# A two-layer decoder on one core: scores for the row maxima on 32x32 tiles of the TensorE array

## The chip, the cores and the metric

The kernel runs on one core of one Trainium2 chip. The metric is the device time of that core in microseconds (us); lower is better. Everything is one program, launched once. TensorE (PE in the profile) multiplies matrices, VectorE (DVE), ScalarE (ACT) and GpSimd (POOL) do the elementwise work, and SyncE (SP) issues DMAs.

## The reference

The input x is 8 sequences of 256 tokens with 512 features. It passes six sublayers, each followed by a layer norm of the sum with its input. Three of them hold causal softmax attention with small heads, and these are the ones that matter here:

```
# layer 0, differential attention: 32 heads of 16 features, keys shared in groups
scores = einsum('bhqd,bhkd->bhqk', q, k) * 16 ** -0.5
scores = where(causal, scores, min);  probs = softmax(scores)
# layer 1, attention: 16 heads of 32 features
scores = einsum('bhqd,bhkd->bhqk', q, k) * 32 ** -0.5      # causal, softmax
# layer 1, last sublayer: 16 query heads of 32 features against one shared key per token
att = einsum('bhqd,bkd->bhqk', q, k_shared) / sqrt(32)     # causal, softmax
```

The other three are a long convolution, a mixture of 8 experts (top 2), and cross attention with 512 features.

## The kernel before

The program has a front stage (layer 0's attention, up to about 460 us), a convolution stage, a middle stage and an experts stage (to about 1199 us), and a tail stage (all of layer 1).

In the front and the tail a softmax is computed in two rounds. First the scores are computed with queries as rows, masked, and VectorE takes the maximum of every row. These maxima are then split into bfloat16 parts, turned, and subtracted by a matmul inside a second computation of the scores, with keys as rows (`scoreT`), whose result ScalarE exponentiates. The first computation serves the maxima alone. It is done by `score(b, n)` in the front, six units for each of the 8 sequences, and by `score(kind, b, c)` in the tail, four units for each sequence in each of two attentions ("P" and "A"), 64 units in all.

A unit fills a PSUM tile `scores` of four banks, `[128, 4, 512]`. Each bank g belongs to one row strip of the array: 32 partitions of q and k, which hold one head (or two of 16 features). Four such strips, each with an operand of 32 partitions, can be in the array side by side, and each writes its own bank. A unit has two steps:

1. `add_masks` (L115 to L123) writes the causal mask with 16 bfloat16 matmuls, for column strip j and row strip g: 32 partitions in, 32 rows out, 256 columns (512 in the front's units n of 4 and 5). This is a tiling of the array in 32x32.
2. The scores are added by fp32 matmuls of 32 partitions in and 128 rows (queries) out, one for each row strip g, a tiling in 32x128. In the front, units n below 4 have four of 512 columns (L335), and units 4 and 5 have two times four of 256 columns (L341). In the tail each unit has four of 256 columns (L1883) and four of 128 (L1886).

The trace has two weight loads and two matmul records for every fp32 matmul of the program, the two passes; a bfloat16 matmul has one of each. Below, a pair is one weight load with its matmul record.

The order of TensorE's work is written out by hand. Between two units stands other work, projections above all (`cols`, `rows`, `query`, `key`; helpers at L191 and L198). The one `scores` tile is claimed through `quads`: a unit waits until VectorE's maxima of the unit before are done (L770 and L774 in the front, L2603 and L2604 in the tail).

Of the kernel before, what the change touches and what calls it, by code (L numbers as in the profile page):

```python
# [13 lines left out]
P = 128  # L14
B = 8
S = 256
# [98 lines left out]
def add_masks(pe, consts, out, copies):  # L115


    for j in range(4):
        for g in range(4):
            rows = slice(32 * g, 32 * g + 32)  # L120
            at = WEDGE + 32 * (g - j)
            part = consts["wedge"][rows, at:at + P].unsqueeze(1).to_broadcast([32, copies, P])
            pe.matmul(out(g, slice(32 * j, 32 * j + 32)), consts["ident_bf"][rows, rows], part, start=True, stop=False,  # L123
                      skip_group_check=True)
# [81 lines left out]
def front_stage(nc, consts, x_in, ctx_in, base_out, vT, cT, w, norm_w, skip, spare, filters, pad_stored, first_traffic, expand, next_traffic,  # L206
# [11 lines left out]
    with ExitStack() as ctx:  # L218
# [62 lines left out]
        def strip(g):  # L281
            return slice(32 * g, 32 * g + 32)
# [13 lines left out]
        with nc.Block() as block:  # L296
            @block.tensor
            def _(pe):
                def drained(key):
                    pe.wait_ge(ring.drained_sem(key), ring.count(key))  # L300
# [24 lines left out]
                def score(b, n):  # L325
                    if n == 0:
                        for j in range(4):
                            drained(("q", b, j))
                        drained(("k", b))
                    bank = quads.claim(pe, ("S", b, n))  # L330
                    q, k = qT[b % 2], kT[b % 2]
                    if n < 4:
                        add_masks(pe, consts, lambda g, rows: bank[rows, g, :].rearrange("p (a k) -> p a k", a=2)[:, :, P:S], 2)
                        for g in range(4):
                            ins = pe.matmul(bank[:, g, :], q[strip(g), n, P:S], k[strip(g)].rearrange("p a k -> p (a k)"),  # L335
                                            start=False, stop=True, skip_group_check=True)
                    else:
                        add_masks(pe, consts, lambda g, rows: bank[rows, g, :].rearrange("p (a k) -> p a k", a=4), 4)
                        for h in range(2):
                            for g in range(4):  # L340
                                ins = pe.matmul(bank[:, g, h * S:(h + 1) * S].rearrange("p (a k) -> p a k", a=2),  # L341
                                                q[strip(g), 2 * (n - 4) + h, 0:P], k[strip(g), :, 0:P], start=False, stop=True,
                                                skip_group_check=True)
                    ins.then_inc(quads.filled_sem(("S", b, n)), 1)

                def shift(b):
# [1373 lines left out]
def tail_stage(nc, consts, region, y_stored, x_in, x_out, y_slots, slot, share, ctx_q, ctx_o, wa, wvo, w, early, early_loaded, cT, ctx_wq, ctx_wo):  # L1720
# [5 lines left out]
    with ExitStack() as ctx:  # L1726
# [87 lines left out]
        def query_of(kind, b):  # L1814
            return q_of.get(b, qT["P"]) if kind == "P" else qT["A"]

        def key_of(kind, b):
            return k_of.get(b, kT["P"]) if kind == "P" else kT["A"]
# [16 lines left out]
        with nc.Block() as block:  # L1835
            @block.tensor
            def _(pe):
                def drained(key):
                    pe.wait_ge(ring.drained_sem(key), ring.count(key))
# [26 lines left out]
                def score(kind, b, c):  # L1866
                    if kind == "P":
                        if c % 2 == 0:
                            drained(("P", "q", b, c // 2))
                            drained(("P", "k", b, c // 2))  # L1870
                        kc = c
                    else:
                        if c == 0:
                            drained(("H", "k4", b))
                        if c % 2 == 0:
                            drained(("H", "q", b, c // 2))
                        kc = 0
                    bank = quads.claim(pe, (kind, "S", b, c))
                    q, k = query_of(kind, b)[:, c], key_of(kind, b)[:, kc]
                    add_masks(pe, consts, lambda g, rows: bank[rows, g, P:3 * P].rearrange("p (a k) -> p a k", a=2), 2)  # L1880
                    for g in range(4):
                        s = slice(32 * g, 32 * g + 32)
                        pe.matmul(bank[:, g, 0:S], q[s, P:S], k[s, 0:S], start=False, stop=False, skip_group_check=True)  # L1883
                    for g in range(4):
                        s = slice(32 * g, 32 * g + 32)
                        ins = pe.matmul(bank[:, g, S:S + P], q[s, 0:P], k[s, 0:P], start=False, stop=True, skip_group_check=True)  # L1886
                    ins.then_inc(quads.filled_sem((kind, "S", b, c)), 1)

                def shift(kind, b):
# [208 lines left out]
                for r in range(2, B):  # L2098
                    p, c, h, a = (r - n if 0 <= r - n < B else None for n in range(4))
# [61 lines left out]
                c, h, a = B - 1, B - 2, B - 3  # L2161
# [74 lines left out]
                for k in range(NC):  # L2236
                    if k < NC - 1:
                        drained(("A", "W", c, k))
                    for t in range(NT):
                        if k == NC - 1:  # L2240
                            pe.wait_ge(half_mixed, t + 1)
                        ins = pe.transpose(banks[t][:, k * P:(k + 1) * P], mixedT[:, k, t * P:(t + 1) * P], consts["ident"][:])
# [746 lines left out]
```

## Time and profile before

| | |
|---|---|
| median of 3 runs | 2129.62 us (2128.32 to 2130.3) |
| span of the profiled execution | 2127.3 us |
| TensorE busy with matmuls | 2057.7 us, 97% of the span |
| TensorE's weight loads | 1194.6 us, 56%, mostly beside the matmuls |
| VectorE | 1128.4 us, 53% |
| ScalarE, GpSimd | 518.8 us, 580.5 us |

The profile is of one execution. A record of a matmul begins when it is let into its part of the array and ends with a modelled end, so records overlap, and the distance from one start to the next start says more than a duration. Tiling and shape stand in a row as `32*128 32x256`: 32 partitions in, 128 rows out, and an operand of 32 partitions by 256 columns that is streamed.

### The profile page before, as it was taken

The numbers are of one execution on the slowest core, as the hardware profiler recorded it, in microseconds if no ns is written. First come the engines' busy times: TensorE is split into PE (matmuls) and PEld (weight loads), VectorE is DVE, ScalarE is ACT, GpSimd is POOL, SyncE is SP. The second block draws the span as 40 slices with busy tenths as digits, with TensorE's granted clock in tenths as the row PEclk, the third lists the DMA queues.
The fourth block names the chain that finished last, engine by engine and source line by source line (L and its number), as shares of the span: only waits on it lengthen the run. The fifth ranks groups of instructions, "written<-read, shape, count | busy, mean of one in ns | idle before, by whom it ended". The sixth has DMA issues, their size and how long they took to land. (4 is left out here: it accounts for less than half of the span.)

```text
span 2127.3 us, 32323 instructions
## 1 busy us (share of the span) xinstructions
PE 2057.7 (97%) x13439; PEld 1194.6 (56%) x13439; DVE 1128.4 (53%) x1731; ACT 518.8 (24%) x791; POOL 580.5 (27%) x548
## 2 busy tenths in 40 slices
PE   7899999999999999999999999999999999999996
PEld 5444444334444557556566655766666666666664
DVE  2567777567777744122222334364646464736567
ACT  2445555440000121101011122122222222222211
POOL 2222222128999600111110312022222222121122
PEclk9999999999999999999999999999999999999998
DMA  5101111205111147321211602100010101000000
GB/s 161 48 1 55 55 56 45 87 38 210 40 43 44 35 156 277 126 65 65 65 65 55 222 3 99 50 31 21 17 44 1 60 1 41 1 31 12 1 11 21
DMA packets 66237, 130.81 MB, mean 61 GB/s; under 512 B 6480, under 2 KB 19920, under 8 KB 66096
## 3 DMA queue, kind: packets, MB, share of 16 engines
q1 hardware_dynamic: 45968, 77.49, 11.1%
q10 hardware_dynamic: 14448, 32.64, 4.3%
q0 software_dynamic: 5680, 18.62, 3.0%
q8 instruction: 111, 1.82, 0.4%
q14 instruction: 30, 0.25, 0.0%
HBM read 97.40 MB, written 41.81 MB: 65 GB/s over the span
## 5 line engine op out<-in xcount | busy, mean ns | idle before, releaser
L1033 PE MATMUL conv_conv<-kv,toep 128*128 128x512 f32 x576 | 247.6, 592 | 0.3 <-POOL kv L1067 0.3
L2615 DVE RECIPROCAL tail_inv<-tail_ring 128x256 f32<-128x256 f32 x63 | 110.7, 1757 | 188.8 <-PE tail_ring L1935 188.3
L1623 PE MATMUL moe_gu_ps<-gu,xT_tile 128*128 x608 | 192.4, 459 | 0.0
L1033 PEld LDWEIGHTS conv_conv<-kv,toep 128*128 128x128 f32 x576 | 109.4, 190 | 139.0 <-issue 129.6
L1067 POOL TENSOR_TENSOR kv<-vT,cT 128x512 f32<-128x512 f32 x128 | 147.0, 1172 | 15.8 <-PE conv_conv L1033 12.0
L2302 POOL TENSOR_TENSOR tail_rstd_x<-tail_rstd_x,const_minus_half 128x2 f32<-128x2 f32 x31 | 21.8, 702 | 469.6 <-DVE tail_rstd_x L2577 469.6
L1623 PEld LDWEIGHTS moe_gu_ps<-gu,xT_tile 128*128 128x128 f32 x608 | 112.3, 190 | 66.5 <-issue 17.8
L2310 POOL TENSOR_SCALAR_AFFINE_SELECT tail_expT<-tail_expT 128x1024 f32<-128x1024 f32 x64 | 71.5, 1119 | 242.1 <-ACT tail_expT L2394 242.0
L2603 DVE TENSOR_REDUCE tail_negtop<-tail_scores 128x4 f32<-128x1024 f32 x64 | 78.2, 1221 | 95.6 <-PE tail_scores L1886 95.4
L594 POOL TENSOR_SCALAR_AFFINE_SELECT front_expT<-front_expT 128x2048 f32<-128x2048 f32 x32 | 64.3, 2008 | 199.1 <-ACT front_expT L649 199.1
L1604 POOL DMA_INDIRECT xg<-x_after,tokens x37 | 35.0, 947 | 282.3 <-PE moe_xT_ps L1618 255.2
L1705 DVE TENSOR_TENSOR moe_hid<-moe_gu_ps,moe_silu 128x352 f32<-128x352 f32 x39 | 20.5, 525 | 170.7 <-PE moe_gu_ps L1623 170.7
L649 ACT ACTIVATE front_expT<-front_scores 128x2048 f32<-128x2048 f32 x48 | 90.1, 1878 | 78.3 <-PE front_scores L367 78.3
L1651 PE MATMUL moe_y_ps<-down,moe_hT 128*128 (+1 forms) x234 | 107.1, 593 | 0.7 <-ACT moe_hT L1691 0.7
L2394 ACT ACTIVATE tail_expT<-tail_scores 128x1536 f32<-128x1536 f32 x63 | 91.4, 1451 | 64.8 <-PE tail_scores L1912 64.8
L1674 ACT ACTIVATE moe_silu<-moe_gu_ps 128x352 f32<-128x352 f32 x39 | 18.1, 464 | 270.2 <-PE moe_gu_ps L1623 270.2
L770 DVE TENSOR_REDUCE front_negtop<-front_scores 128x8 f32<-128x2048 f32 x32 | 73.2, 2288 | 18.6 <-PE front_scores L335 18.4
L2315 POOL TENSOR_TENSOR tail_expT<-tail_expT 128x512 f32<-128x512 f32 x60 | 76.7, 1279 | 5.0
L1089 ACT COPY both<-conv_conv 128x512 f32<-128x512 f32 x32 | 18.7, 586 | 229.9 <-PE conv_conv L1033 211.0
L1717 DVE COPY moe_y<-moe_y_ps 128x512 f32<-128x512 f32 x39 | 27.0, 692 | 72.7 <-PE moe_y_ps L1651 72.7
L198 PE MATMUL tail_ring<-tail_gk,tail_xT 128*128 128x416 f32 (+1 forms) x256 | 63.4, 399 | 1.5 <-ACT tail_xT L2376 1.5
L1651 PEld LDWEIGHTS moe_y_ps<-down,moe_hT 128*128 128x128 f32 (+1 forms) x234 | 41.6, 191 | 38.5 <-issue 38.3
(394 smaller groups left out, 3912.2 us busy)
## 6 DMA issues: line engine op xcount, KB each, us to landing
toep<-toeplitz SPq DMA_DIRECT2D x32, 320.0 KB, 2.9
y_slots<-moe_y ACTq DMA_DIRECT2D x39, 256.0 KB, 2.0
gu<-in_L_ffn_gate_up_proj SPq DMA_DIRECT2D x5, 1408.0 KB, 12.5
toeplitz<-filt_rows SPq DMA_DIRECT2D x8, 768.0 KB
front_e<-in_ctx SPq DMA_DIRECT2D x8, 512.0 KB, 4.7
toeplitz<-filt_rows SPq DMA_DIRECT2D x16, 256.0 KB
x_after<-x SPq DMA_DIRECT2D x8, 512.0 KB, 5.0
tail_x<-x_after SPq DMA_DIRECT2D x8, 512.0 KB, 3.7
```

Source lines behind the costliest of these rows:

```text
L594: pool.affine_select(out=tile, in_=tile, compare_op=ALU.is_ge, fill=0.0, base=0, pattern=[[0, 16], [1, P]], channel_multiplier=-1).then_in ...
L649: act.activation(exp_buf(b, n)[:].rearrange("p g j q -> p g (j q)"), scores[:], ACT.Exp).then_inc(quads.drained_sem(key), 1)
L770: ins = dve.tensor_reduce(negtop[:, 1, n].rearrange("p (g a) -> p g a", a=2), scores[:].rearrange("p g (a k) -> p g a k", a=2), AX_X, ALU. ...
L1033: ins = pe.matmul(bank, toep[p][:, mat * P:(mat + 1) * P], kv[p][:, c].rearrange("p b j i -> p (b j i)"), start=n == 0, stop=n == len(PART ...
L1067: pool.tensor_tensor(kv[p][:, c], tokens_of(c, h), context_of(c, h, 3), ALU.mult).then_inc(kv_ready, 1)
L1623: ins = pe.matmul(gu_ps[:, s % 2, h, 0:HID], (xT if s else mid.xT_first)[:, c, :], wgu[c][:, e, h * HID:(h + 1) * HID], start=c == 0, stop ...
L1651: ins = pe.matmul(y_ps[:, s % 2, :], hT[0:w, n, :], wd[n][0:w, e, :], start=n == 0, stop=n == 2)
L2310: pool.affine_select(out=diagonal, in_=diagonal, compare_op=ALU.is_ge, fill=0.0, base=0, pattern=[[0, 8], [1, P]], channel_multiplier=-1). ...
L2315: pool.tensor_tensor(e[:, 3], e[:, 0], e[:, 2], ALU.add).then_inc(masked[kind], 1)
L2394: act.activation(exp_buf(kind, b, c)[:, 0:3].rearrange("p n g q -> p g n q"), quads.tile(key)[:, :, 0:3 * P].rearrange("p g (n q) -> p g n ...
L2603: dve.tensor_reduce(negtop[:, 1, heads_of(c)], scores[:, :, 0:S], AX_X, ALU.max, negate=True)
L2615: link.after(dve.reciprocal(inv[c % 2][:], bank[:, S:2 * S]))
```

## The change

The scores of step 2 are computed on 32x32 tiles. Each fp32 matmul of 128 queries becomes four of 32 queries each, for column strips j of 0 to 3, with the same streamed operand (the keys) and a quarter of the weights. The order is j outside and g inside, as in `add_masks`. A front unit has 16 matmuls in place of 4 (n below 4) or 32 in place of 8; a tail unit has 32 in place of 8. Masks, `scoreT`, all waits and the work of the other engines are as before.

```diff
                         add_masks(pe, consts, lambda g, rows: ..., 2)
-                        for g in range(4):
-                            ins = pe.matmul(bank[:, g, :], q[strip(g), n, P:S], k[strip(g)].rearrange("p a k -> p (a k)"),
-                                            start=False, stop=True, skip_group_check=True)
+                        for j in range(4):
+                            for g in range(4):
+                                ins = pe.matmul(bank[strip(j), g, :], q[strip(g), n, P + 32 * j:P + 32 * j + 32],
+                                                k[strip(g)].rearrange("p a k -> p (a k)"), start=False, stop=True,
+                                                skip_group_check=True)
...
                         for h in range(2):
-                            for g in range(4):
-                                ins = pe.matmul(bank[:, g, h * S:(h + 1) * S].rearrange("p (a k) -> p a k", a=2),
-                                                q[strip(g), 2 * (n - 4) + h, 0:P], k[strip(g), :, 0:P], start=False, stop=True,
-                                                skip_group_check=True)
+                            for j in range(4):
+                                for g in range(4):
+                                    ins = pe.matmul(bank[strip(j), g, h * S:(h + 1) * S].rearrange("p (a k) -> p a k", a=2),
+                                                    q[strip(g), 2 * (n - 4) + h, strip(j)], k[strip(g), :, 0:P], start=False,
+                                                    stop=True, skip_group_check=True)
...
-                    for g in range(4):
-                        s = slice(32 * g, 32 * g + 32)
-                        pe.matmul(bank[:, g, 0:S], q[s, P:S], k[s, 0:S], start=False, stop=False, skip_group_check=True)
-                    for g in range(4):
-                        s = slice(32 * g, 32 * g + 32)
-                        ins = pe.matmul(bank[:, g, S:S + P], q[s, 0:P], k[s, 0:P], start=False, stop=True, skip_group_check=True)
+                    for j in range(4):
+                        rows = slice(32 * j, 32 * j + 32)
+                        for g in range(4):
+                            s = slice(32 * g, 32 * g + 32)
+                            pe.matmul(bank[rows, g, 0:S], q[s, P + 32 * j:P + 32 * j + 32], k[s, 0:S], start=False, stop=False,
+                                      skip_group_check=True)
+                    for j in range(4):
+                        rows = slice(32 * j, 32 * j + 32)
+                        for g in range(4):
+                            s = slice(32 * g, 32 * g + 32)
+                            ins = pe.matmul(bank[rows, g, S:S + P], q[s, rows], k[s, 0:P], start=False, stop=True, skip_group_check=True)
```

## Rows read from the trace of the kernel before

**Rows 1.** The page: span, and the busy time and instructions of each engine.
```profile
span 2127.3 us, 32323 instructions
PE 2057.7 (97%) x13439; PEld 1194.6 (56%) x13439; DVE 1128.4 (53%) x1731; ACT 518.8 (24%) x791; POOL 580.5 (27%) x548
```
**Rows 2.** Busy time by stretch: PE, PEld, DVE, ACT, POOL, granted clock, DMA share, GB/s.
```profile
0.00:460.00 460.00, 430.43 (x3524) 206.57 (x3525) 286.01 (x361) 213.65 (x274) 99.08 (x91) 0.99 0.20 61
1199.00:2050.00 851.00, 844.25 (x6717) 544.97 (x6715) 440.02 (x714) 193.59 (x275) 177.56 (x165) 1.00 0.10 33
```
**Rows 3.** Timeline of PE, tail unit at 1426 us: start us, length us, line, xcount.
```profile
1426.08 0.33 PE L123 MATMUL tail_scores<-const_wedge,const_ident_bf 32*32 32x256 bf16 x16
1426.34 0.50 PE L1883 MATMUL tail_scores<-tail_kT_a,tail_qT_a 32*128 32x256 f32 x4
1426.66 0.39 PE L1883 MATMUL tail_scores<-tail_kT_a,tail_qT_a 32*128 32x256 f32 x4
1426.87 0.40 PE L1886 MATMUL tail_scores<-tail_kT_a,tail_qT_a 32*128 32x128 f32 x8
1426.98 0.29 PE L1886 MATMUL tail_scores<-tail_kT_a,tail_qT_a 32*128 32x128 f32 x4
1427.20 0.48 PE L191 MATMUL tail_ring<-tail_xT,early_wq 128*128 128x256 f32 x1
```
**Rows 4.** Durations (ns min/median/max) of the masks' and L1883's records, by source line.
```profile
L123 PE MATMUL tail_scores<-const_wedge,const_ident_bf x1024: 264/278/278, 1212.0 to 2097.7; 32*32 32x256 bf16 x171
L1883 PE MATMUL tail_scores<-tail_kT_a,tail_qT_a x256: 374/426/478, 1426.3 to 2098.3; 32*128 32x256 f32 x128
```
**Rows 5.** Timeline of PE, two front units, n of 1 and n of 4.
```profile
237.19 0.33 PE L123 MATMUL front_scores<-const_wedge,const_ident_bf 32*32 32x256 bf16 x16
237.45 1.14 PE L335 MATMUL front_scores<-front_kT,front_qT 32*128 32x512 f32 x8
238.52 1.92 PE L386 MATMUL front_ring<-front_expT,front_v 128*32 128x512 f32 x16
...
249.27 0.43 PE L123 MATMUL front_scores<-const_wedge,const_ident_bf 32*32 32x512 bf16 x16
249.64 1.15 PE L341 MATMUL front_scores<-front_kT,front_qT 32*128 32x256 f32 x16
250.71 0.48 PE L191 MATMUL front_ring<-front_xT,front_wk 128*128 128x256 f32 x1
```
**Rows 6.** Timeline of PE: fp32 on four column tiles, first and second passes.
```profile
2112.06 0.42 PE L1932 MATMUL tail_ring<-tail_expT,tail_v_a 128*32 128x256 f32 x4
2112.30 0.40 PE L1932 MATMUL tail_ring<-tail_expT,tail_v_a 128*32 128x256 f32 x4
```
**Rows 7.** Timeline of PE: a unit after an idle time, with what ended that.
```profile
2056.62 0.33 PE L123 MATMUL tail_scores<-const_wedge,const_ident_bf 32*32 32x256 bf16 x16 [1.01 <-DVE tail_negtop L2604]
2057.41 0.40 PE L1886 MATMUL tail_scores<-tail_kT_a,tail_qT_a 32*128 32x128 f32 x8
```
**Rows 8.** Timeline of PE: first and last of the 12 lines of its densest stretch.
```profile
2108.39 0.86 PE L1932 MATMUL tail_ring<-tail_expT,tail_v_a 128*32 128x256 f32 x16 [0.83 <-POOL tail_expT L2310]
...
2113.16 0.40 PE L1939 MATMUL tail_ring<-tail_expT,tail_ones 128*32 128x128 f32 x8
```
**Rows 9.** Timeline of DVE, then of PE, in the front.
```profile
233.54 0.42 DVE L794 TENSOR_TENSOR front_cross<-front_ring,front_sums 128x256 f32<-128x256 f32 x1 [1.45 <-ACT front_sums L657]
...
234.21 2.29 DVE L770 TENSOR_REDUCE front_negtop<-front_scores 128x8 f32<-128x2048 f32 x1
...
238.92 2.29 DVE L770 TENSOR_REDUCE front_negtop<-front_scores 128x8 f32<-128x2048 f32 x1
...
241.27 0.33 PE L123 MATMUL front_scores<-const_wedge,const_ident_bf 32*32 32x256 bf16 x16 [0.24 <-DVE front_negtop L770]
```
**Rows 10.** Timeline of DVE in the tail, the maxima of one unit.
```profile
1436.96 1.23 DVE L2603 TENSOR_REDUCE tail_negtop<-tail_scores 128x4 f32<-128x1024 f32 x1 [3.02 <-PE tail_scores L1886]
1438.10 0.68 DVE L2604 TENSOR_REDUCE tail_negtop<-tail_scores 128x4 f32<-128x512 f32 x1
```
**Rows 11.** The page: the queue that brings instructions: packets, MB, share.
```profile
q8 instruction: 111, 1.82, 0.4%
```

## The prediction

> **What bounds the kernel now.** I read the page first: TensorE is busy for 97% of the span [rows 1]. Then the windows by stage: in the tail from 1199 to 2050 us it is busy for 844 of 851 us, with VectorE at 440; in the front for 430 of 460 us, with VectorE at 286 [rows 2]. The granted clock is 0.99 to 1.00 in both stretches, the 2.4 GHz level, after unbroken work, and the change takes no work away that could let it fall. So a time that a unit gains on TensorE is a gain of the whole, unless TensorE then stands before a wait. The change touches 48 units in the front and 64 in the tail and nothing else, so the whole question is the length of a unit, and I read one of each kind by the starts of its records.
>
> **A tail unit now** [rows 3]. From the masks' start (1426.08) to the start of the next block (1427.20) it takes 1.12 us:
> - The 16 mask records take 0.33 together and one of them takes 0.28 [rows 3, 4], so their starts lie within 0.05. All 16 tiles run side by side.
> - From the last mask start (1426.13) to the first score record (1426.34): 0.21. This is one pass of the masks, and the emptying of the array before the tiling changes.
> - First passes of L1883 start at 1426.34, second ones at 1426.66: 0.32. Second passes to L1886: 0.21, and this is a pass of 256 columns. So 0.11 of the first interval is weights of 128 columns that nothing covers.
> - L1886's first to its second passes (1426.87 to 1426.98): 0.11, a pass of 128 columns.
> - From there to the next block: 0.22, of which the four starts spread over 0.02, a pass is 0.11, and 0.09 is the array emptying for the next tiling. A masks' pass then also takes 0.21 - 0.09, about 0.11.
>
> **The change part by part.** Removed is the tiling change between masks and scores: 0.09 a unit. Its weights of 128 columns become weights of 32. On four column tiles first passes start 0.24 before second ones [rows 6], so that uncovered weights of 32 columns cost 0.24 - 0.21 = 0.03 and not 0.11; here they can load while the masks stream, so I put them at 0, and 0.03 is the other bound. The columns that are streamed stay the same if all 16 tiles run together: each tile streams what its strip streamed. What is added is pairs. A tail unit has 16 mask pairs and 16 score pairs now; it will have 16 and 64. A front unit with n below 4 goes from 16 and 8 to 16 and 32, one with n of 4 or 5 from 16 and 16 to 16 and 64. In all that is 32 x 24 + 16 x 48 + 64 x 48 = 4608 more pairs to the 13439 that the page shows.
>
> Does the order of the program let 16 tiles run together? For every tile the program gives the first pass, then the second, then goes to the next tile. In the trace the four first passes of L1883 start within 0.50 - 0.48 = 0.02, and the four second ones 0.32 later [rows 3, 4], so a waiting second pass does not hold up the next row strip. The same holds across four column tiles [rows 6]: four starts within 0.02 though each is followed by a waiting second pass. No row has 16 tiles with two passes. I take it that they pass each other there too. Three steps in 0.02 is 0.007 for a tile with two pairs, so 16 tiles start over 0.10, against 0.05 for masks [rows 3]; I take 0.10, as these are fp32, and keep 0.05 as the good end.
>
> The new unit, followed at its last tile:
> - tail: 0.10 spread + 0.11 masks + 0.21 + 0.21 + 0.11 (L1883 twice, L1886's first pass) + 0.20 to the next block = 0.94. Gain 1.12 - 0.94 = 0.18; with a spread of 0.05 it is 0.23.
> - front, n below 4, now 238.52 - 237.19 = 1.33 [rows 5]: 0.10 + 0.11 + 0.43 for 512 columns + 0.52 (0.43 + 0.09) = 1.16, gain 0.17 (0.22).
> - front, n of 4 and 5, now 250.71 - 249.27 = 1.44 [rows 5]: 0.10 + 0.21 + 3 x 0.21 + 0.30 = 1.24, gain 0.20 (0.25).
>
> So 0.18 a unit, and 0.23 at the good end.
>
> **What of it reaches the end.** In the tail VectorE stands idle for 3.02 us before a unit's maxima and waits for TensorE [rows 10], and the maxima themselves take 1.23 + 0.68 us, so they are done long before the next unit claims the tile. Around 2056 TensorE does wait for the maxima [rows 7], but these wait for the scores, so the gain counts there too. All 64 units count: 64 x 0.18 = 11.5 us.
>
> In the front VectorE is nearer. Its cross product starts at 233.54 when ScalarE's sums are there, and the first maxima follow at 234.21, the second at 238.92; TensorE's third unit then waits 0.24 for them [rows 9]. That chain does not move when units 0 and 1 become shorter, so their gain turns into a longer wait at unit 2. From there the maxima wait for the scores or nearly do. I count 3.6 of 6 units in each of six steady sequences, and 11 of the 12 in the first and the last sequence: 33 units, x 0.18 = 5.9 us. The bounds are 24 and 48 units, 4.3 and 8.6 us.
>
> Sum: 11.5 + 5.9 = 17.4 us, from a span of 2127.3 to 2109.9. The median of the runs lies 2.3 above the span, so 2112 us. The good end is 64 x 0.23 + 48 x 0.23 = 25.8 us, 2104. On the other side the gain of this case could be half, 2121.
>
> **Rivals.**
> 1. *Too few pairs a microsecond* (slower). A tail unit now starts 32 pairs in about 0.9 us, also after an idle time, 29 ns a pair [rows 7]; the masks alone start 16 in 0.05, 3 ns a pair. The new unit wants 80 in 0.94, 12 ns a pair, and the turning point is 1.12 / 80 = 14 ns. The densest long stretch has 116 pairs (12 lines) from 2108.39 to 2113.29, 42 ns a pair [rows 8], but there the streams set the pace, so the rows only bound the rate from one side. At 29 ns a tail unit takes 2.3 us, +1.2 x 64 = 77, the front units of 80 pairs +0.9 x 16 = 14, those of 48 pairs stay: 2220. At 20 ns, 1.6 us: +0.48 x 64 + 0.16 x 16, less 0.17 x 22 for the others: +30, 2160. The instructions come by a queue that moved 1.82 MB [rows 11]; a third more pairs make it 2.4 MB, which at 0.4% of the engines is nothing unless a burst outruns it. For the rival: nobody has tried more than 32 such pairs in a row. Against: the 3 ns, also straight after an idle microsecond. Chance 0.15, a third of it below 2150. The Trainium skill (TensorE: Matmul & The Clock Gate, section "Wait — 56ns, not 53.3ns?") says that from one matmul's start to the next there are never less than about 25 ns. By that a tail unit would take 80 x 25 = 2.0 us and the kernel some 2190. The masks' starts in this trace do not agree with it, at 3 ns [rows 3, 4].
> 2. *Order within a row strip* (slower). If a waiting second pass holds up the next column tile of the same row strip, the strip runs first of j=0; second of j=0 with first of j=1; and so on: five intervals where two stood. For L1883 and L1886 together that is 4 x 0.21 + 5 x 0.11 = 1.4 in place of 0.64, so a tail unit is 0.05 + 0.11 + 1.39 + 0.09 = 1.64, +0.5 x 64 = 33. Front: 5 x 0.43 + 0.25 = 2.4, +1.05 x 32 = 34, and 9 x 0.21 + 0.35 = 2.3, +0.8 x 16 = 13. Together +80: 2209. It speaks for it that every row with two passes has four tiles alone; against it that neither four row strips nor four column tiles behave so. Chance 0.12. The same page of the Trainium skill (section "Part 3: Packing small matmuls — row/col tiling") says that matmuls keep their program order in start and end; by that rows 3 could not have four first passes before any second one, so the trace disagrees.
> 3. *Weights no longer covered* (about even). Four weight loads of 0.03 for the column tiles of one strip, one after another and beside no pass, are 0.12, at four passes 0.48, and a unit is 0.94 + 0.48 = 1.4 at worst; a half of that gives 1.18, +0.06 x 64 + 0 in the front, 2133. Places between the forecast and 2145 belong here. Chance 0.13. Rows 6 speak against it, where 0.03 is all that shows.
>
> **How the numbers follow.** Forecast 0.60, at 2112; rivals 0.15, 0.12, 0.13. The range of 2104 to 2150 holds the forecast's 0.60, all of the third rival and a third of the first, 0.78; it reaches no further up, since the next case is at 2160 to 2220. A measurement of this kernel can tell some 0.2% (4 us) from no change. Faster by more: 0.60 and a little of the third, 0.62. Within: 0.08. Slower: 0.30.
>
> **What would show it.** Right: masks and scores of a tail unit start within 0.75 of each other with no gap of 0.2 between L123 and the scores, and the next block starts 0.94 after the masks (0.89 to 0.98). Records of first passes lie on 16 tiles within 0.10. First rival: starts of pairs in even steps of more than 12 ns, and the unit's length proportional to its pairs, so that front units of 48 pairs gain and those of 80 lose. Second: second passes interleave with first passes of the next j at steps of 0.21. In the front the wait at the third unit for the maxima grows from 0.24 to about 0.6. The prediction is wrong if units come out longer than 1.12 in the tail, whatever the reason.

## The result and the profile after

The changed kernel takes 2149.27 us (median of 4 runs, 2144.56 to 2151.27) where the kernel before took 2129.96 in the same session (4 runs). The ratio is 1.0095, with a 95% interval of 1.0082 to 1.0108: it is slower by 19.3 us. The forecast was 2112, a gain of 17.4. The time lies just inside the range of 2104 to 2150, but the sign is wrong.

The page of the changed kernel, the lines that answer to [rows 1, 11]: span, busy time and count of each engine, and the queue that brings instructions.

```profile
span 2146.5 us, 41539 instructions
PE 2078.1 (97%) x18047; PEld 1212.3 (56%) x18047; DVE 1127.5 (53%) x1731; ACT 518.6 (24%) x791; POOL 579.7 (27%) x548
...
q8 instruction: 147, 2.41, 0.5%
```

The pairs grew by 18047 - 13439 = 4608, the number that was counted. The span grew by 19.2 us and TensorE's busy time by 20.4. Its idle time up to its last matmul, all gaps added up, went from 61.6 to 60.3 us. So no new wait for another engine took the gain: units became longer inside. The two stretches say the same as [rows 2], at the same granted clock (columns as there; the stretches are shifted by the later start of the tail, and the first is 10 us longer):

```profile
0.00:470.00 470.00, 440.24 (x5068) 214.34 (x5068) 289.81 (x363) 215.99 (x277) 100.01 (x92) 0.99 0.19 60
1202.00:2069.00 867.00, 860.09 (x9486) 556.17 (x9484) 441.46 (x715) 193.56 (x274) 177.13 (x165) 1.00 0.10 33
```

A tail unit, a front unit with n below 4 and one with n of 4 or 5, in the timeline of PE (start us, length us, line, xcount), to be set beside [rows 3, 5]. L1888 is the old L1883, L1894 the old L1886, L336 and L344 the old L335 and L341:

```profile
1442.20 0.33 PE L123 MATMUL tail_scores<-const_wedge,const_ident_bf 32*32 32x256 bf16 x16
1442.32 0.77 PE L1888 MATMUL tail_scores<-tail_kT_a,tail_qT_a 32*32 32x256 f32 x25
1442.75 0.27 PE L1894 MATMUL tail_scores<-tail_kT_a,tail_qT_a 32*32 32x128 f32 x1
1442.76 0.47 PE L1888 MATMUL tail_scores<-tail_kT_a,tail_qT_a 32*32 32x256 f32 x7
1442.94 0.72 PE L1894 MATMUL tail_scores<-tail_kT_a,tail_qT_a 32*32 32x128 f32 x31
1443.58 0.48 PE L191 MATMUL tail_ring<-tail_xT,early_wq 128*128 128x256 f32 x1
...
238.63 0.33 PE L123 MATMUL front_scores<-const_wedge,const_ident_bf 32*32 32x256 bf16 x16
238.75 1.34 PE L336 MATMUL front_scores<-front_kT,front_qT 32*32 32x512 f32 x32
240.02 0.64 PE L389 MATMUL front_ring<-front_expT,front_v 128*32 128x512 f32 x4
...
250.84 0.43 PE L123 MATMUL front_scores<-const_wedge,const_ident_bf 32*32 32x512 bf16 x16
251.06 1.55 PE L344 MATMUL front_scores<-front_kT,front_qT 32*32 32x256 f32 x64
252.54 0.48 PE L191 MATMUL front_ring<-front_xT,front_wk 128*128 128x256 f32 x1
```

From the masks' start to the next block is 1443.58 - 1442.20 = 1.38 us where it was 1.12; 1.39 where it was 1.33; and 1.70 where it was 1.44. These are also the medians over all units:

| unit | count | before | after | change |
|---|---|---|---|---|
| tail | 64 | 1.123 | 1.382 | +16.6 us together |
| front, n below 4 | 32 | 1.333 | 1.391 | +1.9 |
| front, n of 4 and 5 | 16 | 1.441 | 1.702 | +4.2 |

Together 22.7 us, which is 3.5 more than the span grew by. Most of that rest lies outside the units. From the end of the last front unit to the start of the first tail unit, where nothing was changed, the profiled execution of the changed kernel is 2.7 us shorter (791.9 us, before 794.6). The two traces differ there in the granted clock: the one of before has stretches at 0.50, the 1.2 GHz level, at 479 and 762 us, where the changed kernel's shows 1.00; at 400 us it is the other way round. That is a difference of two executions and not the work of the change. Inside the tail, from the first unit's start to the last one's, the time grew by 16.0 us (885.7 to 901.7), and the 63 units in it give 63 x 0.259 = 16.3.

The tiling change did go. The first scores start at 1442.32, 0.07 after the last mask start (1442.25), where 0.21 stood before. The loss comes right behind. The same timeline in five narrow stretches that end at 1442.49, .51, .53, .545 and .63. The count is that of the records of L1888 let in by then, since none of them has ended yet (they last 0.37):

```profile
1442.32 0.40 PE L1888 MATMUL tail_scores<-tail_kT_a,tail_qT_a 32*32 32x256 f32 x8
...
1442.32 0.56 PE L1888 MATMUL tail_scores<-tail_kT_a,tail_qT_a 32*32 32x256 f32 x9
...
1442.32 0.60 PE L1888 MATMUL tail_scores<-tail_kT_a,tail_qT_a 32*32 32x256 f32 x10
...
1442.32 0.62 PE L1888 MATMUL tail_scores<-tail_kT_a,tail_qT_a 32*32 32x256 f32 x15
...
1442.32 0.70 PE L1888 MATMUL tail_scores<-tail_kT_a,tail_qT_a 32*32 32x256 f32 x24
```

Eight tiles start between 1442.32 and 1442.35 and then no matmul starts for 0.16 us, until 1442.51. The single records, in ns from the masks' start: masks at 0 to 52; first passes of tiles 0 to 7 at 122 to 145, 3.3 apart; first passes of tiles 8 to 15 at 307, 324, 341, ... 424, 16.65 apart; second passes of tiles 0 to 7 at 337 to 361, of tiles 8 to 15 at 522, 562, ... 662. L1894 repeats it: the first pass of its tile 0 at 553, then no matmul of L1894 until 739, where the second pass of tile 0 starts; first passes of tiles 1 to 8 at 747 to 864, in steps of 16.7; of tiles 9 to 15 at 931, 972, 989, ... 1056; its last pass at 1187; the next block at 1384. (The zero is the first weight load of the masks; the first mask itself starts at 2.)

### The profile page after: what moved, and what is told of

The parts are those of the page before. It is cut to its first block and busy times, and to the rows that moved or that the text cites. A ratio compares the mean times of both kernels' runs of the same rounds, so it can differ in the third digit from the quotient of the medians.

```text
span 2146.5 us, 41539 instructions
## 1 busy us (share of the span) xinstructions
PE 2078.1 (97%) x18047; PEld 1212.3 (56%) x18047; DVE 1127.5 (53%) x1731; ACT 518.6 (24%) x791; POOL 579.7 (27%) x548
## 3 DMA queue, kind: packets, MB, share of 16 engines
q8 instruction: 147, 2.41, 0.5%
## 5 line engine op out<-in xcount | busy, mean ns | idle before, releaser
L1708 DVE TENSOR_TENSOR moe_hid<-moe_gu_ps,moe_silu 128x352 f32<-128x352 f32 x39 | 20.4, 524 | 170.7 <-PE moe_gu_ps L1626 170.7
```

## The theories and the experiments

What stops tiles 8 to 15? Two theories were put on trial.

- **Window.** TensorE holds 64 records, weight loads and matmuls counted alike, from the time they are let in until they and all before them have ended. 16 masks are 32 records and 8 tiles with two passes are 32 more. The matmul of tile 8 has to wait for the first mask to end: it ends at 280, and tile 8 starts 27 ns later. That weight loads hold places too, and that places come free in program order, is seen in the same unit. The 65th record, the weight load of tile 8, starts at 129, when the first weight load has ended (87). The weight loads of all masks have ended by 138, but no record behind the 65th comes in until the first mask has ended too. In the other units the numbers fit as well: with masks of 512 columns (first end at 387) tile 8 starts at 415, and L1894's tile 0 starts its second pass at 739, 28 after tile 0's second pass of L1888 has ended (337 + 374 = 711).
- **Supply.** A burst stands ready, and behind it the instructions come at a fixed pace, 16.65 ns for a tile with two pairs, whatever ran before. This is the first rival of the prediction in its milder form.

The profile of before has a sign that may belong here and that I had not read: the sequencer's own wait instruction (L99, listed by source line). In the unit at 237.19, which has 48 records, it comes at 237.3, before the unit's scores have started; in the unit at 249.27, which has 64, it comes at 249.7, 0.45 us after the masks' start:

```profile
L99 PEldq EVENT_SEMAPHORE  x1: 51/51/51, 237.3 to 237.3; - x1
...
L99 PEldq EVENT_SEMAPHORE  x1: 51/51/51, 249.7 to 249.7; - x1
```

In the tail it mostly comes 0.28 us after the start of units with 64 records, 0.07 with 48 (x6 below) and 0.02 with 32 (x3 below). But the sign isn't clean. In x6 the front's units n of 4 have 48 records, and it comes only at 0.39; in x5 front units of 64 records have it at 0.10. So it also depends on something else than the number of records, and nothing below rests on it.

**The pairs alone (x1_probe).** In one place of the tail, before one unit, long rows of matmuls on 16 tiles in turn are added to the kernel before: bfloat16 with 16, 128 and 256 columns, 128 of each, and fp32 with 16, 64, 128 and 256 columns, 96 of each. They write to the tile that the unit then clears.

```diff
+                        def half16(r, s, g, n):
+                            pe.matmul(bank[r, g, 0:n], consts["ident_bf"][s, s], consts["wedge"][s, 0:n], start=True, stop=True, skip_group_check=True)
...
+                        def full16(r, s, g, n):
+                            pe.matmul(bank[r, g, 0:n], q[s, r], k[s, 0:n], start=True, stop=True, skip_group_check=True)
...
+                        lots(8, 16, half16)
+                        lots(8, 128, half128)
...
+                        lots(6, 256, full256)
```

> The kernel before, with matmuls on 32x32 tiles added in the tail ahead of the first unit, 16 tiles in turn, in long rows without a gap; their output is written over by the masks. Theory W (window): TensorE holds 64 records at most (weight loads and matmuls), each from when it is let in until it and all before it have ended; a record takes its place 0.03 us after one is free. Theory S (supply): after a first burst records come at a fixed pace, four in 16.7 ns, whatever is in flight. Start to start of one tile's turn to the next. bf16, one pair a tile, 16 and 128 columns: both 8 ns. bf16, 256 columns (a record lasts 278 ns): W (278 + 27) / 32 = 9.5, S 8.3. fp32, two pairs a tile, 16 columns: both 17. 64 columns: W 19, S 17. 128 columns: W (107 + 268 + 27) / 16 = 25, S 17. 256 columns: W (213 + 374 + 27) / 16 = 38, S 26.7, which is the stream alone.

Measured: 2160.77 us, one run. The row of 16 columns shows both parts by itself. Timeline of PE, at 1211.90, and at 1211.95 to 1212.00:

```profile
1211.84 0.24 PE L1889 MATMUL tail_scores<-const_wedge,const_ident_bf 32*32 32x16 bf16 x21
...
1211.84 0.29 PE L1889 MATMUL tail_scores<-const_wedge,const_ident_bf 32*32 32x16 bf16 x32
```

There are 21 pairs after 0.07 us and 32 after 0.12, and there it stays. The first record lasts 178 ns, and the matmul of the 33rd pair starts at 205, 27 ns behind its end. From then on pairs start 8.3 ns apart. So the stop after 32 pairs is there without any tiling change, mask or fp32, and the pace of a refill is 8.3 ns against 3.3 ns for pairs that stand ready. Rows of 128 bfloat16 columns keep the 8.3 (133 ns for 16 pairs).

The longer rows can't be set beside the expectation as it stands. It was worked out with record lengths of the 2.4 GHz level, and the probe fell to the other one. TensorE had stood idle for 1.61 us just before (the pauses are told at the end), and from 1216.5 to 1240.4 us the granted clock was 0.50, which is 1.2 GHz. Three windows of the probe, with the clock in the third column from the end, and the record lengths (ns min/median/max) of the rows of 64 and 128 fp32 columns, which lie in the second window:

```profile
1211.80:1216.40 4.60, 2.78 (x242) 2.21 (x242) 0.00 (x0) 0.60 (x1) 3.66 (x4) 1.00 0.33 80
1216.60:1240.30 23.70, 14.21 (x784) 10.77 (x786) 0.00 (x0) 0.00 (x0) 0.95 (x1) 0.50 0.12 32
1240.40:1243.60 3.20, 2.85 (x152) 1.97 (x127) 0.00 (x0) 0.00 (x0) 0.00 (x0) 1.00 0.00 0
...
L1901 PE MATMUL tail_scores<-tail_kT_p,tail_qT_p x192: 259/309/312, 1224.9 to 1232.3; 32*32 32x64 f32 x192
L1904 PE MATMUL tail_scores<-tail_kT_p,tail_qT_p x192: 367/415/419, 1232.2 to 1237.6; 32*32 32x128 f32 x192
```

With the lengths of this level, and passes twice as long, both theories can be worked out again, for the stretches between the pauses:

| row | window | supply | measured |
|---|---|---|---|
| fp32, 64 columns, at 0.50 | (107 + 309 + 27) / 16 = 28 ns a tile | 17 | 27 to 28 |
| fp32, 128 columns, at 0.50 | (213 + 415 + 27) / 16 = 41 | 27 | 40.5 |
| fp32, 256 columns, at 1.00 | 38, as expected | 27 | 39 to 41 |
| bfloat16, 256 columns, at 0.50 | (367 to 417 + 27) / 32 = 12 to 14 ns a pair | 13, the stream alone | 12 to 14 |

So the window has the size of all four, and the supply theory misses the three fp32 rows by a third or more. The bfloat16 row does not tell the two apart. The fp32 row of 16 columns took 19 ns a tile, where both had 17. In the bfloat16 rows there are also four shorter stops of 0.24 to 0.30 us which neither theory has.

**The small tiles without the masks (x2_fine_no_masks).** The changed kernel without its masks; the scores start the group themselves. This kernel's result lacks the masks.

```diff
-                        add_masks(pe, consts, lambda g, rows: bank[rows, g, :].rearrange("p (a k) -> p a k", a=2)[:, :, P:S], 2)
...
-                                                k[strip(g)].rearrange("p a k -> p (a k)"), start=False, stop=True,
+                                                k[strip(g)].rearrange("p a k -> p (a k)"), start=True, stop=True,
```

> The changed kernel without the masks of the maxima: add_masks is left out in all 112 units, the first scores start the accumulation. W: a tail unit's 64 records of L1888 fit at once, its 16 first passes start within 0.10; the records of the 128 columns wait for the first tile's second pass to end (0.61 after the start), and the unit is 1.2 us from its first record to the next block. S: 24 pairs at once and 40 at 8.3 ns are in after 0.41, so that the streams alone are left, 0.85 us. A front unit with n below 4 (64 records): both 1.1.

**The row strips without the masks (x3_row_no_masks).** The same edit on the kernel before, as the other side of the comparison. It too leaves the masks out.

> The kernel before without the masks of the maxima, as in x2. Both theories: a unit loses its masks and the tiling change, 0.26 in the tail, so 0.86 us; front 1.07 for n below 4 and 1.07 for n of 4 and 5. It is the measure for x2: by W fine tiles are slower than this in the tail (1.2), by S the same (0.85).

Measured: 2133.17 and 2103.30 us, one run each (before: 2129.21). A tail unit takes 1.211 us on small tiles and 0.865 on row strips; front units with n below 4 take 1.083 and 1.071, with n of 4 or 5 1.424 and 1.076. Window had 1.2 for the small tiles in the tail, supply 0.85. The two runs are 30 us apart, and the lengths of the units alone give 64 x 0.346 + 16 x 0.348 + 32 x 0.012 = 28. A tail unit of the run on small tiles, from the timeline of PE:

```profile
1424.15 0.71 PE L1885 MATMUL tail_scores<-tail_kT_a,tail_qT_a 32*32 32x256 f32 x32
1424.61 0.82 PE L1891 MATMUL tail_scores<-tail_kT_a,tail_qT_a 32*32 32x128 f32 x32
1425.36 3.72 PE L191 MATMUL tail_ring<-tail_xT,early_wq 128*128 128x256 f32 x16
```

Now the first 16 tiles have the window to themselves, and they do what the prediction wanted: all 16 first passes start within 0.10 us, 6.7 ns apart, and the second ones follow in the same order 0.24 later. But the 64 records of L1885 (16 tiles with four) fill the window, and now L1891 pays: its first pass of tile 0 starts at 0.458, and then nothing until 0.643, 27 ns after the second pass of L1885's tile 0 has ended (242 + 374 = 616). So the masks as such aren't the cause: whatever comes behind 64 records waits for the end of the first of them.

**Tiles of 32x64 (x4_tiles_32x64).** Half the number of tiles: two column tiles of 64 queries for each row strip. A tail unit has 16 masks and 32 score pairs.

```diff
-                    for j in range(4):
+                    for j in range(2):
                         for g in range(4):
-                            pe.matmul(bank[rows, g, 0:S], q[s, P + 32 * j:P + 32 * j + 32], k[s, 0:S], start=False, stop=False,
+                            pe.matmul(bank[r, g, 0:S], q[s, P + 64 * j:P + 64 * j + 64], k[s, 0:S], start=False, stop=False,
```

> Scores on 32x64 tiles: two column tiles of 64 queries for each row strip, so half the added pairs; the masks stay on 32x32 and the tiling change stays. W: after the masks have drained, the 64 records of a tail unit's scores fit at once; the uncovered weights are 64 columns and not 128, so a tail unit is 1.12 - 0.05 + 0.03 (spread) = 1.10 us and the time is 2126 to 2130. S: 32 pairs, 24 at once and 8 at 8.3 ns, the same. If only the number of pairs counted, as in the first rival of the prediction, half of the loss, 2139.

Measured: 2127.23 us (10 runs, 2122.89 to 2130.5), ratio 0.9988 (0.9978 to 0.9997). Tail units take 1.094, front units 1.306 and 1.415:

```profile
1426.38 0.33 PE L123 MATMUL tail_scores<-const_wedge,const_ident_bf 32*32 32x256 bf16 x16
1426.64 0.69 PE L1887 MATMUL tail_scores<-tail_kT_a,tail_qT_a 32*64 32x256 f32 x16
1427.12 0.42 PE L1892 MATMUL tail_scores<-tail_kT_a,tail_qT_a 32*64 32x128 f32 x16
```

The masks with L1887's 8 tiles are just 64 records, and nothing is held up between them. The change of tiling is back (0.21 from the last mask to the first score), and what is gained is uncovered weights: from first to second passes of L1887 it is 0.27 us, where [rows 3] had 0.32 with weights of 128 columns. The kernel is faster than before by a tenth of a per cent. Both theories had this size, so the run does not tell them apart. But it rules out that each added pair has a price of its own. A tail unit has 16 added pairs here against 48 in the change, which is a third and not the half of the expectation. A third of the loss would have been 2136 us, and there is none.

**The front alone (x7_front_alone).** The change in the front, the tail as before.

> The change in the front alone; the tail as before. By the lengths of the units in the changed kernel (1.33 to 1.39 for n below 4, 1.44 to 1.70 for n of 4 and 5) the front loses up to 32 x 0.06 + 16 x 0.26 = 6 us, less where VectorE bounds it: 2132 to 2135. The tail alone would then hold the other 64 x 0.26 = 17 us. If a third more pairs cost something outside the units, through the instruction queue, the two parts would not add up to the measured 19 us.

Measured: 2134.14 us (10 runs, 2129.2 to 2137.98), ratio 1.0029 (1.0018 to 1.0040), some 6 us slower than before; front units 1.390 and 1.700, tail units 1.123. The front's share by unit lengths is 1.9 + 4.2 = 6.1 us, so in the front about the whole length of the units reaches the end. The tail holds the other two thirds: 19.3 - 5.9 = 13 us, against 16.6 by its units, with an uncertainty of some 4 us (an estimate from the two intervals) on the difference of two sessions. The profile of the changed kernel, with the tail grown by 16.0 us, speaks for the larger figure.

**One pass in place of two (x5_upper_fine and x6_upper_row).** If pairs are what counts, the maxima can do with fewer. The maximum only shifts the exponent of the softmax and falls out of the quotient, so the scores for it may be computed with the upper halves of q and k, read as bfloat16 in place: one pass and one pair. `scoreT` stays in fp32. In x5 this is done on the small tiles of the changed kernel (a tail unit has 32 score pairs in place of 64), in x6 on the row strips of before (8 in place of 16).

```diff
+def upper(m):
+    """The upper halves of float32, as bfloat16, in place."""
+    names = " ".join("abc"[:len(m.shape) - 2])
+    return m.bitcast(BF16).rearrange(f"p {names} (n two) -> p {names} n two", two=2)[(slice(None),) * (len(m.shape)) + (1,)]
...
-                    q, k = qT[b % 2], kT[b % 2]
+                    q, k = upper(qT[b % 2][:]), upper(kT[b % 2][:])
```

> The changed kernel with the scores of the maxima computed from the upper halves of the fp32 numbers of q and k, read in place as bf16 with a step of two: one pass and a bf16 stream in place of two fp32 ones. The maxima are only shifts of the softmax, both in its numerator and its denominator. A front unit with n below 4 now has 16 + 16 pairs, 64 records. W: they all fit the window, so nothing waits for masks to end: 0.5 us (1.39 in the changed kernel). A tail unit has 48 pairs; the 16 of 128 columns enter from 0.31 on at 8.3 ns each: 0.6 us. Front n of 4 and 5: 0.75. W for the comparison with x6: fine tiles win where the unit fits the window (n below 4, 0.5 against 0.69), and are about even in the tail. Time 2072 to 2082.

> The kernel before (row strips, tiling change) with the same upper halves as in x5. Tail unit: 0.26 masks and tiling change + weights 0.11 or less + 0.11 + 0.05 + 0.11 = 0.58 to 0.64 us. Front 0.69 for n below 4 and 0.79 for n of 4 and 5. Tail: 0.5 x 64 = 32 us less; front 0.65 x 48 = 31, of which half or less arrives, as VectorE's maxima (2.29 us) bound the chain there. Time 2080 to 2087.

Measured: 2082.20 us (ratio 0.9781, 0.9764 to 0.9797) and 2081.09 us (0.9775, 0.9759 to 0.9792), four runs each. Both are 2.2% faster than the kernel before, and so faster than the changed one as well. The units of x5 have the lengths that the window theory gave (0.50, 0.58 and 0.75 us, expected 0.5, 0.6 and 0.75); its time is just above the expected range of 2072 to 2082. The small tiles are the test of the window here. Timeline of PE in x5, a tail unit and a front unit with n below 4:

```profile
1631.28 0.33 PE L129 MATMUL tail_scores<-const_wedge,const_ident_bf 32*32 32x256 bf16 x16
1631.40 0.32 PE L1894 MATMUL tail_scores<-tail_kT_a,tail_qT_a 32*32 32x256 bf16 x16
1631.58 0.35 PE L1900 MATMUL tail_scores<-tail_kT_a,tail_qT_a 32*32 32x128 bf16 x16
1631.86 0.70 PE L197 MATMUL tail_ring<-tail_xT,tail_wk 128*128 128x256 f32 x2
...
230.03 0.33 PE L129 MATMUL front_scores<-const_wedge,const_ident_bf 32*32 32x256 bf16 x16 [1.06 <-DVE front_negtop L779]
230.15 0.44 PE L342 MATMUL front_scores<-front_kT,front_qT 32*32 32x512 bf16 x16
230.51 0.64 PE L395 MATMUL front_ring<-front_expT,front_ones 128*32 128x512 f32 x4
```

In the front unit masks and scores are 32 pairs together. All 16 scores start within 0.055 us (119 to 174 ns) and the unit takes 0.49 us (0.50 in the median); on row strips (x6) it takes 0.60. This is the one kind of unit where the idea of the change pays. In the tail unit the third group of 16 is over the window: it starts at 305 ns, the first mask's end (278) + 27, in steps of 8.3, and the unit takes 0.583 where the row strips take 0.545. My sizes for x6 were off by up to 0.09: its units came out shorter than expected. And the units' gain was not all kept: in x6 TensorE waits for the maxima of the front's unit before for 11.8 us, where it was 4.5:

```profile
PE front_scores L129 <- DVE front_negtop L776: 11.8, 18, 1.6
```

**Small tiles only where they fit (x8_upper_mixed, with x9_upper_row_again beside it).** x6 with the small tiles of x5 in the front's units with n below 4.

```diff
-                        for g in range(4):
-                            ins = pe.matmul(bank[:, g, :].rearrange("p (a k) -> p a k", a=2), q[strip(g), n, P:S], k[strip(g)],
+                        for j in range(4):
+                            for g in range(4):
+                                ins = pe.matmul(bank[strip(j), g, :].rearrange("p (a k) -> p a k", a=2), q[strip(g), n, P + 32 * j:P + 32 * j + 32],
+                                                k[strip(g)],
```

> Row strips and upper halves as in the kernel of the sixth run, but the front's units with n below 4 on 32x32 tiles: 16 masks and 16 scores are 32 pairs and fit the window of 64 records. Window theory: these 32 units take 0.49 us as in the fifth run, the two of 80 pairs... the front units n of 4 and 5 stay at 0.71 and the tail units at 0.545. 32 x 0.11 = 3.4 us on TensorE, of which the front's maxima take back half or more: 1 to 2 us faster than the row strips alone, 2079 to 2080. A supply that sets the pace after a burst expects the same units at 0.60 or longer and the time the same or higher. 2078 to 2081 in all.

> The kernel of the sixth run again, on the same chip as the mixed one, so that the two can be set beside each other: 2080 to 2082, 1 to 2 us above the mixed one by the window theory, no difference or below it if small tiles cost something elsewhere.

Measured: 2081.49 us (5 runs, 2076.89 to 2082.08; ratio 0.9768, 0.9755 to 0.9781) and 2082.78 (5 runs, 2080.61 to 2085.09; 0.9784, 0.9770 to 0.9797). The 32 units take 0.49 us (median) as expected, against 0.60, but the intervals of the two overlap, and a gain of 1 to 2 us in the whole is neither shown nor excluded. The windows and waits of the two say why it must be small. First stretch of x8 and of x9, then the wait for the maxima in each:

```profile
0.00:470.00 470.00, 417.45 (x3712) 199.30 (x3713) 304.94 (x387) 217.97 (x281) 109.25 (x101) 0.99 0.21 67
...
PE front_scores L129 <- DVE front_negtop L778: 13.2, 18, 1.7
```

```profile
0.00:470.00 470.00, 421.09 (x3328) 201.05 (x3329) 305.04 (x387) 217.96 (x281) 109.38 (x101) 0.99 0.21 67
...
PE front_scores L129 <- DVE front_negtop L776: 10.4, 17, 1.3
```

TensorE is busy 3.64 us less in the front, about 32 x 0.11, and waits 2.8 us longer for VectorE. In these kernels the front hangs on VectorE's maxima.

## Why the prediction was wrong, step by step

**What bounds the kernel: right.** TensorE's units are what counts, in both stages: the longer units reached the end almost whole (19.3 of 22.7 us; inside the tail's trace 16.0 of 16.3), and the kernels with shorter ones won 2.2%.

**The tiling change (0.09 a unit) and the weights: right in kind.** The gap from masks to scores fell from 0.21 to 0.07, a saving of 0.14 in which 0.05 of the weights' 0.11 is contained. The 0.03 that I kept as a bound for uncovered weights of 32 columns shows too: some 23 ns for each late tile, in records of 396 or 397 ns where those covered last 374:

```profile
L1888 PE MATMUL tail_scores<-tail_kT_a,tail_qT_a x1024: 371/374/397, 1432.3 to 2117.3; 32*32 32x256 f32 x171
```

**The step that failed** is the term for the spread of the starts, "so 16 tiles start over 0.10", on which every unit of the sum rests. It came from "No row has 16 tiles with two passes. I take it that they pass each other there too". That they pass each other was right: x2 shows the spread of 0.10 to the digit when the 16 tiles are all that is in flight. What I left out is that a tile stands in line behind what was let in before it. The prediction counted columns and starts; it never counted how many records are in TensorE at once. In place of one spread of 0.10, the runs show two waits for a whole record, and a tail unit of 1.38 us where the sum had 0.94. Followed at its last tile, with the measured numbers, it is:

- 0.31 until tile 8 may start (a mask's record, 0.28, and 0.03), where the sum had 0.11 masks and half of 0.10
- 0.21 for its first pass, as in the sum
- 0.41 until L1894's tile 9 may start: the second pass of L1888's tile 8 must have ended (0.374 for the record, and 0.03); the sum had 0.21, since it thought a pass, not a record, stands before it
- 0.13 from tile 9 to tile 15 (one step of 0.04, which L1888's second passes of tiles 8 and 9 have too, and five of 0.017); the sum had 0.05
- 0.13 for a pass of 128 columns with its uncovered weights; the sum had 0.11
- 0.20 to the next block, as in the sum.

Together 1.38 (before rounding). A record of 256 columns lasts 0.374 us but a pass occupies its tile for 0.21 only; held in the window, it costs its whole length. These lengths were there to be read [rows 4], and I used them for nothing but intervals. The ends of records are modelled by the profiler, so the lengths are only as good as that; what speaks for the theory is that the starts that follow come 27 or 28 ns behind ends of four different lengths (178, 278, 385 and 374 ns).

**The rivals.** The first (too few pairs a microsecond) has the right sign and a sign of its own that came true in part: 80-pair units lose most. But its condition was wrong. It wanted even steps of more than 12 ns and front units of 48 pairs that gain. The steps are 3.3, a stop, and then 8.3 ns a pair, below the turning point of 14 that I had worked out; and the units of 48 pairs lose 0.06. The price is that of the stops. The 25 ns between starts that the Trainium skill gives (TensorE: Matmul & The Clock Gate, section "Wait — 56ns, not 53.3ns?") is seen nowhere among tiles: 3.3 ns standing ready, 8.3 in a refill. The second rival (order within a row strip) is refuted: tiles 4 to 7, the second column tile of each row strip, start their first passes at 135 to 145, long before any second pass (337 to 361). The third (weights no longer covered) is real but small, the 23 ns above. The measured 2149 lies just above its upper end of 2145 and in the third of the first rival that I had put below 2150, so the range held by luck: neither mechanism was the one that cost the time.

**The front's third unit** was to wait 0.6 for the maxima where it had waited 0.24. It waits 0.21, since the units before it did not get shorter:

```profile
242.75 0.33 PE L123 MATMUL front_scores<-const_wedge,const_ident_bf 32*32 32x256 bf16 x16 [0.21 <-DVE front_negtop L773]
```

What the forecast got right there shows in x6 and x8, where the units did get shorter and the wait for the maxima grew to 10 to 13 us.

**What I could have weighed.** The Trainium skill (TensorE: Matmul & The Clock Gate, section "The mechanism") gives TensorE a reorder window 64 deep, and speaks of it only as what pulls weight loads ahead. The runs here agree with the 64, at 32 pairs in x1 and at 8 tiles behind 16 masks. Its table in "Measured speedup vs the span model" has 16 tiles side by side with a speedup of 10.6; no run here measures that figure. A pack of 16 pairs fits twice into the window, while the unit here has 80.

**What stays open.** Whether the sequencer or the array keeps the 64 places no run tells. Nor does one tell what sets the 8.3 ns of a refill, or the four short stops of the probe. And of the 3.5 us that the units' 22.7 exceed the span's growth by, about 1 is not placed.

## What to carry to other kernels

Before a matmul is cut into more and smaller ones, count the records (a weight load and a matmul each, two of both for fp32) that stand in a row: up to 64, with those of the step before, run side by side, and the next waits for the end of the first, at the whole length of its record. In this kernel small tiles pay where masks and scores together are at most 32 pairs (0.49 us against 0.60), and cost where they are more (1.38 against 1.12). Where a score only serves a maximum that falls out again, one pass on the upper halves in place of two in fp32 is worth far more than any tiling tried here: 2.2%.

## What the runs showed of the hardware that was not expected

- 64 records in flight, let go in program order, and a place taken up again 27 or 28 ns after it comes free (x1, and the units of every kernel here).
- Two paces: 3.3 ns a pair for pairs that stand ready, 8.3 ns in a refill; an fp32 tile with two pairs accordingly 6.7 and 16.65 ns.
- Long bursts of small matmuls seem to run the instructions dry. In x1 TensorE stands idle eight times, for 1.1 to 2.2 us six times and for 0.2 and 0.4 in the rows of 256 fp32 columns, always 128 pairs (256 records) apart, with nothing waited for. The first two:

```profile
1213.08 1.45 PE L1892 MATMUL tail_scores<-const_wedge,const_ident_bf 32*32 32x128 bf16 x80
1216.14 0.86 PE L1892 MATMUL tail_scores<-const_wedge,const_ident_bf 32*32 32x128 bf16 x48 [1.61 <-issue]
1216.74 1.58 PE L1895 MATMUL tail_scores<-const_wedge,const_ident_bf 32*32 32x256 bf16 x80
1220.42 0.93 PE L1895 MATMUL tail_scores<-const_wedge,const_ident_bf 32*32 32x256 bf16 x48 [2.10 <-issue]
```

  From one pause to the next are 48 + 80 = 128 pairs. From the end of one pause to the end of the next it is 3.5 to 4.3 us in all rows alike. The page suggests why this number of pairs: the change added 9216 records and 2.41 - 1.82 = 0.59 MB to the instruction queue, 64 bytes a record, and a packet of the queue is 2.41 MB / 147 = 16.4 KB, so 256 records. The units of the changed kernel, with other work between bursts of 80 pairs, show no such pause. No run here varied the fetch, so the cause is argued from the sizes. The Trainium skill (Runtime: NRT & Kernel Launch, section "Instruction fetch mechanics") has instructions brought in blocks of 16 KiB, 256 instructions, and says that the cost is mostly hidden; the size agrees, but in these bursts, if the pauses are the fetch, it is not hidden.
